# Gated cross-attention and a routed expert layer on one core: the routing's vector work in another order, router weights split inside the first batch, and the last stage's sums taken in PSUM

## The reference, cut to what matters

```python
x = x + tanh(g_xattn) * xattn(layernorm(x), ctx, wq, wk, wv, wo)   # x: (4, 512, 512)
x = x + tanh(g_ffn)   * ffn(layernorm(x), Wg, W1, W2, W3, W1s, W2s, W3s)

def xattn(x, ctx, ...):            # 4 batches of 512 rows, keys and values: ctx and x itself
    q, k_new, v_new = x @ wq, x @ wk, x @ wv
    k, v = concat(ctx, k_new), concat(ctx, v_new)
    return softmax(q @ k.T / sqrt(512)) @ v @ wo

def ffn(x, ...):                   # 2048 tokens of 512
    shared = (silu(x @ W1s.T) * (x @ W3s.T)) @ W2s.T               # width 704
    probs = softmax(x @ Wg.T)                                      # 16 experts
    topk_w, sel = top_k(probs, 4)
    h = silu(x @ W1[e].T) * (x @ W3[e].T)                          # width 352
    routed = sum over the 4 chosen e of topk_w * (h @ W2[e].T)
    return shared + routed
```

## Time and profile before

| | |
|---|---|
| time, median of 3 runs | 1065.23 us (1064.37 to 1068.74) |
| the profiled execution's own time | 1068.17 us |
| its span, first to last instruction | 1066.5 us |
| mean granted TensorE clock | 0.992 of full |
| busy: TensorE, VectorE, ScalarE, GpSimd | 96%, 59%, 37%, 48% |
| chain that ended last: TensorE, GpSimd, VectorE, DMA | 82%, 7%, 5%, 2% |
| stages in the trace | attention to 398 us, first shared products to 508 us, experts to 960 us, combining to the end |

### The profile page before, as it was taken

How to read it: one execution, slowest core, us unless ns; L and a number is a source line. 1 busy time by engine, 2 the same in 40 slices (tenths; PEclk the granted TensorE clock), 3 DMA queues, 4 the chain that set the end, 5 groups by cost and what they waited for, 6 DMA issues and landing times.

```text
span 1066.5 us, 18142 instructions
## 1 busy us (share of the span) xinstructions
PE 1027.4 (96%) x5211; PEld 886.9 (83%) x5212; DVE 626.4 (59%) x1112; ACT 390.2 (37%) x708; POOL 514.5 (48%) x545
## 2 busy tenths in 40 slices
PE   5999999999999999899999999999999999999994
PEld 4878877887888877687899999999999999998883
DVE  3253466448445556886765556555655565556777
ACT  4431132123213213232554555455545554552120
POOL 5620202010220062103888888866766766645775
PEclk9999999999999999999999999999999999999998
DMA  8050475439137429413675555554555455546797
GB/s 329 28 159 19 179 237 158 150 98 315 27 143 250 156 101 343 123 58 124 188 221 169 184 172 177 173 182 165 174 169 179 167 175 168 183 154 236 229 293 229
DMA packets 80254, 186.23 MB, mean 175 GB/s; under 512 B 11552, under 2 KB 32160, under 8 KB 76960
## 3 DMA queue, kind: packets, MB, share of 16 engines
q1 hardware_dynamic: 53184, 117.26, 33.7%
q0 software_dynamic: 16672, 49.70, 14.6%
q10 hardware_dynamic: 10368, 18.88, 4.8%
HBM read 149.10 MB, written 49.28 MB: 186 GB/s over the span
## 4 chain that ended last, share of the span: by engine, by line
PE 82%; POOL 7%; DVE 5%; issue 3%; DMA 2%; ACT 2%; SPq 0%; POOLq 0%; DVEq 0%; ACTq 0%
PE c_ps_u L89 26%; PE ps_products L89 23%; PE c_ps_y L89 14%; PE ps_scores L89 8%; POOL parts L1791 6%; PE b_ps_u L89 4%; PE c_ps_h L1691 2%; PE ps_transposed L700 1%; PE b_ps_y L1023 1%; ACT tile_hot L1250 1%; DMA wq_raw<-wq 1%; DMA parts<-y_dram,token_slots 1%; DVE pT_lo L494 0%; PE ps_products L755 0%; DVE row_max L516 0%
## 5 line engine op out<-in xcount | busy, mean ns | idle before, releaser
L1473 POOL DMA_INDIRECT xs<-xn_dram,column x288 | 302.6, 1051 | 86.7 <-issue 81.7
L89 PE MATMUL c_ps_u<-expert_hi,xT_hi 128*128 x576 | 191.9, 333 | 0.0
L89 PE MATMUL c_ps_u<-expert_hi,xT_lo 128*128 x576 | 185.5, 322 | 0.0
L89 PE MATMUL c_ps_u<-expert_lo,xT_hi 128*128 x576 | 184.8, 321 | 0.0
L1646 DVE TENSOR_TENSOR expert_lo<-stage,expert_hi 128x1088 f32 x72 | 93.3, 1295 | 65.8 <-ACT expert_hi L1597 52.3
L89 PEld LDWEIGHTS c_ps_u<-expert_lo,xT_hi 128*128 128x128 f32 x576 | 108.9, 189 | 0.0
L89 PEld LDWEIGHTS c_ps_u<-expert_hi,xT_hi 128*128 128x128 f32 x576 | 108.0, 188 | 0.0
L89 PEld LDWEIGHTS c_ps_u<-expert_hi,xT_lo 128*128 128x128 f32 x576 | 107.9, 187 | 0.0
L1659 DVE TENSOR_TENSOR hf<-c_ps_u,gate 128x352 f32<-128x352 f32 x72 | 37.8, 525 | 109.9 <-ACT gate L1588 109.9
L1597 ACT ACTIVATE expert_hi<-stage 128x1088 f32 x72 | 80.3, 1116 | 20.8 <-issue 20.8
L89 PE MATMUL c_ps_y<-expert_hi,hT_lo 128*128 (+1 forms) x216 | 85.4, 395 | 0.0
(11 more groups left out here) (295 smaller groups left out, 2380.0 us busy)
## 6 DMA issues: line engine op xcount, KB each, us to landing
stage<-we SPq DMA_DIRECT2D x76, 544.0 KB, 3.7
y_dram<-y ACTq DMA_DIRECT2D x72, 256.0 KB, 2.1
xs<-xn_dram,column POOLq DMA_INDIRECT x288
ctxT_raw<-ctxT SPq DMA_DIRECT2D x4, 1024.0 KB, 6.5
ctx_raw<-ctx SPq DMA_DIRECT2D x4, 1024.0 KB, 4.8
r_t<-x SPq DMA_DIRECT2D x4, 1024.0 KB, 5.3
x_dram<-r_t SPq DMA_DIRECT2D x4, 1024.0 KB, 4.3
out<-total SPq DMA_DIRECT2D x16, 256.0 KB, 4.5
```

The lines of the kernel that those rows point to most:

```text
L89: last = pe.matmul(out, a[i], b[j], start=(n == 0), stop=(n == 3 * len(pairs) - 1))
L1473: pool.indirect_dma_start(xs[:, g, :], None, rows, bass.IndirectOffsetOnAxis(ap=sources[:, g:g + 1], axis=0)).then_inc(sem, 16)
```

## The change

- The split of the router's weights moves into the first batch: ScalarE's half ahead of the first `exps(0)`, VectorE's between `maxima(0)` and `maxima(1)`.
- GpSimd makes the routing's constants (`consts`, nine small instructions) behind the routing's first memset instead of in the attention stage, ahead of the load of the first expert's high halves.
- The routing's pieces stand elsewhere: the four `choose` at places 6, 7, 8, 9 instead of all at 5, `slots` at 9, `hot_tiles` at 9 and 10 (before 11, 12), `hot_rows` at 11 and 12 behind `schedule` (before 9, 10, 13), `hot_tokens` at 11 and 12 (before 13, 14).
- `list_slots` moves from ahead of up step (1, 5) to the middle of up step (1, 4); `turn_sources` from ahead of down step (1, 0) to ahead of up step (1, 5). `found_tokens` stays behind up step (1, 4).
- In the expert stage, `turn_h(0)` moves between the two halves of tile 1's up products.
- In combining, ScalarE copies `total` into one of two PSUM banks (`lift`), VectorE sums there and writes the last of the four to SBUF; `combine` c stands at other places.

```diff
 attention, ScalarE: attend(b)
-            if b is not None:
+            if b is None:
+                act.wait_ge(small_in, 48)
+                act.activation(wg_both[:, :, :, 0:E], wg[:], ACT.Copy).then_inc(wg_hi, 1)
+            else:
                 m.up(2)
 attention, ScalarE, behind attend(None)
-        act.wait_ge(small_in, 48)
         act.activation(gates[:], gates[:], ACT.Tanh).then_inc(gate_ready, 1)
-        act.activation(wg_both[:, :, :, 0:E], wg[:], ACT.Copy).then_inc(wg_hi, 1)
 attention, VectorE: attend(b)
             maxima(0)
-            if b is not None:
+            if b is None:
+                dve.wait_ge(wg_hi, 1)
+                dve.tensor_tensor(wg_both[:, :, :, E:2 * E], wg[:], wg_both[:, :, :, 0:E], ALU.subtract).then_inc(wg_split, 1)
+            else:
                 split_r(b)
 attention, VectorE, behind attend(None)
-        dve.wait_ge(wg_hi, 1)
-        dve.tensor_tensor(wg_both[:, :, :, E:2 * E], wg[:], wg_both[:, :, :, 0:E], ALU.subtract).then_inc(wg_split, 1)
 attention, GpSimd
         split_up(1)
-        consts()
         root(var2, rstd2, 2 * B)
 routing, GpSimd
                            pattern=[[1, E], [-1, E]], channel_multiplier=0).then_inc(const_ready, 1)
+        consts(pool)
         load_expert(pool, later.w_hi, 0, io, 0, hi_in["first"])
 routing, ScalarE
-        work = {1: last_rows, 2: router, SC + IT + 3: lambda: hot_tokens(0), SC + IT + 4: lambda: hot_tokens(1)}
+        work = {1: last_rows, 2: router, SC + IT + 1: lambda: hot_tokens(0), SC + IT + 2: lambda: hot_tokens(1)}
 routing, VectorE
-        work = {0: (last_rows,), 1: (logits, shifted, softmax, larger_), 2: (equals, added, choices), 4: (counts,), 5: (slots,),
-                9: (lambda: hot_rows(0, piece), lambda: hot_rows(piece, piece)),
-                10: (lambda: hot_rows(2 * piece, piece), lambda: hot_rows(3 * piece, piece)),
-                11: (lambda: hot_tiles(0),), 12: (lambda: hot_tiles(1),), 13: (schedule,),
+        work = {0: (last_rows,), 1: (logits, shifted, softmax, larger_), 2: (equals, added, choices), 4: (counts,),
+                6: (lambda: choose_slot(0),), 7: (lambda: choose_slot(1),), 8: (lambda: choose_slot(2),),
+                9: (lambda: choose_slot(3), slots, lambda: hot_tiles(0)), 10: (lambda: hot_tiles(1),),
+                11: (schedule, lambda: hot_rows(0, piece), lambda: hot_rows(piece, piece)),
+                12: (lambda: hot_rows(2 * piece, piece), lambda: hot_rows(3 * piece, piece)),
                 14: (found_tokens,), 15: (source_rows, places, slices, lambda: first_low(0)),
 routing, TensorE: ahead(n, k)
-            if at == LIST_AT:
-                list_slots()
-            if at == LIST_AT + 1:
+            if at == SC + IT + 5:
                 turn_sources()
 routing, TensorE: amid(n, j)
+            if (n, j) == (1, 4):
+                list_slots()
 experts, TensorE: step(t, v)
-            if later_than(t, 0):
+            if later_than(t, 1):
                 turn_h(t - 1, 1 - u)
 ...
             for k in range(2):
+                if k and isinstance(t, int) and t == 1:
+                    turn_h(0, 0)
 combining
+    ps_sum = sh.ps_t[:].rearrange("p u k n -> p u (k n)")
+    first = SC + IT
+    at = [2, 3, SC - 2, SC - 1, SC, SC + 1, SC + 2, SC + 3,
+          *(first + k for k in (1, 2, 3, SC - 2, SC - 1, SC + 1, SC + 2, SC + 3))]
-        at = [2, 3, SC - 1, SC, SC + 1, SC + 2, *(first + k for k in (0, 1, 2, 3, SC - 1, SC, SC + 1, SC + 2, SC + 3, SC + 3))]
 combining, ScalarE; behind(n, k) calls lift(c) where at[c] - 1 == n * first + k, behind that step's silu and high
+        def lift(c):
+            k, before = place(order[c])
+            act.wait_ge(total_in[k], before * 16 + 16)
+            if c >= 2:
+                act.wait_ge(summed, (c - 1) * TOPK)
+            act.activation(ps_sum[:, c % 2, :], total[k][:], ACT.Copy).then_inc(base_up, 1)
 combining, VectorE: combine(c)
-            dve.wait_ge(total_in[k], before * 16 + 16)
+            dve.wait_ge(base_up, c + 1)
-                ins = dve.scalar_tensor_tensor(out=total[k][:], in0=parts[c % 4][:, q, :],
+                acc = ps_sum[:, c % 2, :]
+                ins = dve.scalar_tensor_tensor(out=total[k][:] if q == TOPK - 1 else acc, in0=parts[c % 4][:, q, :],
                                                scalar=keep["weights"][:, order[c], q:q + 1],
-                                               in1=total[k][:], op0=ALU.mult, op1=ALU.add)
+                                               in1=acc, op0=ALU.mult, op1=ALU.add)
```

More of the change, by code:

```diff
@@ L304, in sync, with gpsimd @@
         return lambda: sp.wait_ge(t_ready, 8 * B + 8)
-    def gpsimd(pool, consts):
+    def gpsimd(pool):
         pool.memset(half[:], -0.5).then_inc(const_ready, 1)
@@ L884 @@
 PIECES = 4
-LIST_AT = SC + IT + 5
 class Later:
@@ L1041, in tensor, with scalar @@
                 down(n, i)
-    def scalar(self, act, ahead=lambda n, j: None):
+    def scalar(self, act, ahead=lambda n, j: None, behind=lambda n, k: None):
         def high(n, j):
@@ L1057, in scalar @@
                     high(n, j - 1)
+                if j < SC - 1:
+                    behind(n, j)
             high(n, SC - 1)
+            for k in range(SC - 1, SC + IT):
+                behind(n, k)
             if n == 0 and not self.apart:
@@ L1218, in consts @@
         pool.iota(token_i[:], [[P, NT]], base=0, channel_multiplier=1).then_inc(made, 1)
-        pool.wait_ge(made, 5)
+        pool.wait_ge(made, 6)
         pool.memset(f["afresh"][:, :, 0:1], 0.0).then_inc(const_ready, 1)
@@ L1229, in gpsimd @@
         pool.memset(lower[:], 1.0).then_inc(made, 1)
-        pool.wait_ge(made, 6)
+        pool.wait_ge(made, 1)
         pool.affine_select(out=lower[:], in_=lower[:], compare_op=ALU.is_gt, fill=0.0, base=0,
                            pattern=[[1, E], [-1, E]], channel_multiplier=0).then_inc(const_ready, 1)
+        consts(pool)
         load_expert(pool, later.w_hi, 0, io, 0, hi_in["first"])
@@ L1287, in count, with choose @@
             keep["cum"] = e_f["cum"]
-        def choose(what, out):
-            for k in range(TOPK):
+        def choose(what, out, ks=range(TOPK)):
+            for k in ks:
                 then(dve.scalar_tensor_tensor(out=f["one"][:], in0=keep["ranks"][:], scalar=float(k),
@@ L1294, in choose, with choose_slot @@
                 then(dve.tensor_reduce(out[:, :, k], f["one"][:], AX.X, ALU.add))
+        def choose_slot(k):
+            choose(f["slot"][:].rearrange("p e j -> p j e"), slot_f, (k,))
         def slots():
-            choose(f["slot"][:].rearrange("p e j -> p j e"), slot_f)
             then(dve.tensor_copy(keep["slots"][:], slot_f[:]))
@@ L1357, in equals @@
         def equals():
-            dve.wait_ge(const_ready, 5)
+            dve.wait_ge(const_ready, 1)
             equal_()
@@ L1464, in tensor @@
         sh.tensor(pe, lambda: pe.wait_ge(keep["up_ready"], 2), down_ready_and_free, ahead, amid)
-    return sync, gpsimd, scalar, vector, tensor, consts
+    return sync, gpsimd, scalar, vector, tensor
 def gather_sides(pool, mem, xs, sources, sem):
@@ L1736, in combining_phase @@
     total_in, total_out = ([sem(f"total{k}_{n}") for k in range(2 * IT)] for n in ("in", "out"))
-    summed = sem("summed")
+    summed, base_up = sem("summed"), sem("base_up")
     out_d = out.rearrange("(n p) d -> n p d", p=P)
@@ L1808, in ahead, with behind @@
                     sh.high(act, 1, i)
-        sh.scalar(act, ahead)
+        def lift(c):
[4 more added lines that the diff above has]
+            act.activation(ps_sum[:, c % 2, :], total[k][:], ACT.Copy).then_inc(base_up, 1)
+        def behind(n, k):
+            for c in range(NT):
+                if at[c] - 1 == n * first + k:
+                    lift(c)
+        sh.scalar(act, ahead, behind)
     def vector(dve, second_free, weights):
@@ L1838, in next_rows @@
                 sh.low(dve, 1, i)
-        first = SC + IT
-        at = [2, 3, SC - 1, SC, SC + 1, SC + 2, *(first + k for k in (0, 1, 2, 3, SC - 1, SC, SC + 1, SC + 2, SC + 3, SC + 3))]
         def between(n, k):
@@ L1891, in _ @@
         def _(pool):
-            attention[1](pool, lambda: routing[5](pool))
+            attention[1](pool)
             routing[1](pool)
```

## The result

The kernel after takes 1062.30 us, the median of 16 runs (1057.97 to 1068.15); the kernel before, run beside it, 1065.56 (16 runs). The ratio is 0.9969, interval [0.9955, 0.9982]: 3.3 us or 0.3% faster. In a second session it was 0.9950 [0.9934, 0.9966], 5.3 us. Forecast were 7.6 us and 1057.6. The time lies in the forecast's range, but the gain is 0.43 of what was forecast in one session and 0.70 in the other, and a time between 1059.9 and 1070.6 had been given a chance of 0.26. Ratios, and the median of c_routing, are of undisturbed executions; among those left out, one of c_routing took 1731.86 us at a granted clock of 0.56.

The account below looks back on a forecast made before the run. TensorE was taken to bound most of the kernel, gathers and VectorE's sums its end. Terms 3.4 - 0.4 + 0 + 4.6 = 7.6 us off the 1065.23 median gave 1057.6 us, range 1052.5 to 1063 (8 in 10).

Parts of the forecast that it names:

- Router weights: At the loop's door: 2.1 us wait and 1.6 us of slow clock go, 0.3 stays; 3.4 us gained.
- Constants and routing: Constants on GpSimd: zero; routing: 5.4 us gained at the third down step, 5.8 given back at the turn, 0.4 lost.
- Expert tile 1: Expert stage: the 1.1 us wait before tile 1's products moves to tile 0's low halves; gain 0, at most 1.1.
- Gathers and PSUM sums: Combining: sums in PSUM at 0.75 us each stop delaying GpSimd, so the 64 gathers end 8.2 us sooner.
- The step that failed: Last stage's store-and-load chain: tile 11's total lands about 1035.5, so ScalarE's copy delays up step (1, 4)'s silu 0.3 us.
- rival 4: Combining: the store-and-load chain now holds ScalarE and so TensorE; 1.3 us more a hop eats the gain; chance 0.06.
- S: Follow-up theory, not in the prediction: in most executions a half-clock stretch follows one of combining's waits for `d_h_lo`.
- The baseline: The sum: 7.6 us off the profiled span of 1066.5, then taken off the median of 1065.23, giving 1057.6 us.
- the combining: Last stage: TensorE ends 3.1 us later, but fewer sums follow it; 4.7 us gained, 4.6 taken.

Follow-up runs that it names:

- c_routing: The kernel before with only the routing's part of the change, including the constants on GpSimd: 1066.82 us, ratio 1.0003 to the kernel before.
- after_again: The kernel after, unchanged, run again for a second profile: 1062.40 us, ratio 0.9950 to the kernel before.
- d_combining: The kernel before with only the combining's part (ScalarE's copies into PSUM, sums there, new places): 1065.05 us, ratio 0.9992 to the kernel before.
- fix_list: The kernel after with the list back ahead of up step (1, 5) and the turn ahead of down step (1, 0): 1055.15 us, ratio 0.9885.
- d_places_alone: The kernel before with only the combines' new places, sums still in SBUF: 1066.04 us, ratio 0.9985 to the kernel before.
- load_sooner_b: The kernel after with SyncE's load of the total for place 14 issued one hop sooner: 1059.02 us, ratio 0.9937 to the kernel before.

## Why the prediction was wrong

**Router weights: right in sum, by another split.** The wait went and no wait stayed at the door (0.3 was taken). Over the six profiles with this door it is 2.1 to 3.2 us, 2.7 on average, and a slow stretch followed it in one. So 2.7 + 1.6/6 = 3.0 would have been the better working, though the 3.4 lies nearer to the 4.0 measured; both lie within its interval, 2.6 to 5.5.

**Constants and routing: right.** First half: up step (1, 0) starts 51.3 us after the first up product (394.31 to 445.63) for 57.1 before, 5.8 for 5.4. Second half: 3.7 for 3.9, and the stretch of 1.6: up step (1, 5) takes 4.41 us to the next step's first product (480.92 to 485.33) for 2.86 before. Sum 0.3 for 0.4, by a measurement that runs from 2.0 slower to 1.4 faster.

**Expert tile 1: as forecast in the trace** (1.02 for 1.1 waited at the next place), not shown by a time.

**Gathers and PSUM sums: right.** The 64 gathers take 63.3 us, 6.9 less for some 8.2 forecast, and end out of the way; a PSUM sum costs what it costs in SBUF. In the trace before, 29 gathers start while a sum runs and take 1.22 us on average; after, 28 do and take 0.945. The 1.3 us that is missing comes from the splits L1074, both inputs in SBUF: seven gathers beside them take 1.26 each, so more stays than the 1.5 that was forecast. The rule of the Trainium skill, "SBUF — State Buffer", section "Who interferes with whom", fits: GpSimd is no longer held when the sums have one SBUF input. With the places kept this part gives its 3.3 us.

**The step that failed: "by one hop of that chain less the issues (4.8, an estimate from the 5.4 below), lands at about 1035.5, and the copy takes 0.6: 0.3 lost".** It took the time of one load from a chain in which nothing hung on it. After the change ScalarE's copy, the silu, VectorE's product and low halves and TensorE's second down stage hang on it in that order, so it is no longer its usual time that counts but its late ones. In the profile shown it cost 0.65 us, near enough; in after_again 2.87, then a wait of 3.5 for 1.7 and a stretch of 2.6: a tail of 76.1 for 71.3. Of the table's four profiles of kernels with this copy, its load in the old order and combines at places 4 and 14, two (d_combining, after) have tails of 71 and two (after_again, fix_list) of 76, where the four with the last stage as before have 74.2 to 75.1. So the part loses in the one form and gains in the other. The means of four, 73.7 and 74.6, differ by 0.9 us, which is what the part measured, 0.9 for 4.6; but four profiles do not show how often each form comes. That is rival 4's mechanism, given 0.06 because I priced it only as a chain that is late on the whole, not as one that is late in some executions. Issuing that one load a hop sooner returns 3.3 us of the medians (2.4 by the mean of the two ratios of after, 1.4 by the second alone). Together with the 0.9 that is 2.3 to 4.2 us of the 4.6 forecast.

**A smaller part is S.** The waits themselves, 1.6 and 1.7 by the rows, were forecast as 1.7 and 1.1; they move TensorE's end to 65.0 us after the first down product for 60.9, 4.0 for 3.1. A stretch at half clock behind one as short as 1.9 is seen once (d_places_alone), and behind none of the six waits of 1.5 to 1.7 for `d_h_lo` in the four profiles of after, after_again, d_combining and fix_list. How often it comes in the kernel after is open.

**The baseline.** 7.6 us was taken off the span of one execution and then off a median. Its span, 1066.5, was 1.8 above the mean of 35 further runs (1064.7). This didn't mislead by itself: the parts' ratios add up to 4.0 - 0.3 + 0.9 = 4.6, within both measurements of the whole. Of the missing 3.0 us the combining lacks 3.7; the router's weights gave 0.6 more and the routing 0.1.

## What to carry to other kernels

When a change puts an instruction that waits for a DMA ahead of work that feeds the bounding engine, price that DMA by its late landings, and compare runs' spans with the profile's before trusting a tail read from one execution. Move the transfer before moving the work: one exchanged line on SyncE returned 1.4 to 3.3 us. And a queue order may be good on one engine and bad on another: VectorE's new order was worth 5.8 us once the list and the turn stayed where TensorE had them; with no combine at places 4 and 14 besides, the kernel takes 1050.9 us (fix_both), 1.5% less than before.

## What the runs showed of the hardware that was not expected

The length of a wait does not alone decide whether TensorE's clock falls to half behind it. In the profiles of the table all 15 waits of 3.5 us or more behind the kernel's start (the third down step six times, the turn seven, `d_h_lo` twice) were followed by a stretch at 0.50. In the same profiles, of those between 1.9 and 3.2 us, three were (1.91 in d_places_alone, 2.10 in before, 2.58 in load_sooner_b) and nine were not, the 3.17 above among them. What the stretches cost differs too: 1.6 us at the turn, 2.6 in after_again.

The landing of one plain load of 256 KB differs as well: from issue to the copy that waits for it 4.7 us in after, 5.0 in fix_list, 6.5 in after_again; and from one load of the chain to the next it takes 4.6 to 7.6 us.
